# GpSimd takes over the block sums of two edge passes, ScalarE copies them out of PSUM, VectorE takes over the value products

## The chip, the cores and the metric

The kernel runs on one core of a Trainium2 chip. The metric is the device time of one execution in microseconds (us), as the median of several runs. A core has TensorE (PE, with its weight loads shown apart as PEld), VectorE (DVE), ScalarE (ACT), GpSimd (POOL) and SyncE (SP), which here only issues DMAs. The engines run side by side and wait for each other on semaphores.

## The reference, cut to what matters

Four graph layers run over 6250 nodes with 128 channels and 200000 edges. Two of their steps matter here. The attention layer (called gat) computes for every edge

```
e = leaky_relu(a_src[src] + a_dst[dst]);  e = exp(e - m[dst])      # 4 heads
s = segment_sum(e, dst);  out = segment_sum(h[src] * e, dst)      # later divided by s[dst]
```

and the transformer layer (called value in its last step) computes

```
attn_exp = exp(attn - max)                                        # 8 heads
attn_sum = segment_sum(attn_exp, row);  out = segment_sum(attn_exp * v[col], row)
```

so each pass multiplies a gathered row of 128 channels by a weight per head, and sums rows and weights by node.

## The kernel before

The edges are sorted by node and padded so that a group of 256 edges (two tiles of 128, one edge to a partition) belongs to a single block of 128 nodes. There are NG = 832 groups. The function `pass_phase` makes one pass over them. It is called four times, with kind "max", "gat", "logit" and "value"; the change touches the kinds "gat" and "value" alone. In these two the gathered rows were written to DRAM by an earlier pass, and SyncE loads them back in order, four tiles (a quarter of a ring of 16 tiles, two groups) at a time. A quarter is loaded again once `matched` tells that its groups of the round before are through TensorE.

Each engine runs its own loop over the groups, written out 8 groups to an iteration (`turns`). A stage with a lag of 3 works in turn J on group J-3. The order of the stages in the list is the order on the engine, and nothing is reordered. Per group:

- DVE makes two one-hot tiles of 128x128 by comparing a ramp with the node numbers (`make_hot`, L1495).
- In gat, PE turns them (`turn`, L1442), ACT copies them out of PSUM (`turn_hot`, L1404), PE looks up the values of the destination node (`look`, L1452), and four small DVE steps make the score: `sum_scores` L1536, `lean_scores` L1541, `lower_scores` L1546, `bound_scores` L1553. ACT takes the exponential (`exp_scores`, L1408) and DVE multiplies the rows by it (`message`, L1560). PE also runs one matmul whose result nobody reads (`idle`, L1482).
- In value, ACT copies the finished weights beside the rows (`weights`, L1413) and GpSimd multiplies the rows by them (`message`, L1381).
- PE multiplies one-hot by rows (`multiply`, L1476) and leaves a block's 128x132 (gat) or 128x136 (value) sums of this group in a PSUM bank. There are 2 banks for this in gat and 4 in value (`sum_ring`).
- DVE adds the bank to the accumulator `k.acc` in SBUF, at the columns of the group's block (`add`, L1505). It reads the block's number from a table into a register for that (L1293). TensorE waits on `added` before it uses a bank again.

The order on each engine before is: in gat, DVE sum_scores, message, lean_scores, make_hot, lower_scores, add, bound_scores; ACT exp_scores, turn_hot; PE multiply, idle, look, turn. In value, DVE make_hot, add; ACT weights; GpSimd message; PE multiply.

Of the kernel before, what the change touches and what calls it, by code (L numbers as in the profile page):

```python
# [1245 lines left out]
def pass_phase(nc, k, name, which, table, row, kind):  # L1246
# [75 lines left out]
    def wait(eng, sem, count):  # L1322

        if not (isinstance(count, int) and count <= 0):
            eng.wait_ge(sem, count)
# [8 lines left out]
    def ring(j):  # L1334
        return G * (j % GB)


    used = {"logit": scored}.get(kind, matched)

    with nc.Block() as block:  # L1340
        def load_quarter(sp, i, q):
# [31 lines left out]
        @block.gpsimd  # L1373
        def _(pool):
            def message(g, i, j):

                arrived(pool, i, j)
                pool.wait_ge(weighed, g + 1)
                rows = k.gat[:, ring(j):ring(j) + G, 0:C].rearrange("p t (h c) -> p t h c", h=H2)
                wts = k.gat[:, ring(j):ring(j) + G, C:C + H2].unsqueeze(3).to_broadcast([P, G, H2, D2])  # L1380
                pool.tensor_tensor(rows, rows, wts, ALU.mult).then_inc(ready, 1)  # L1381

            if kind == "value":
                turns(pool, [(0, message)])
                return
            if from_lists:
                return
            for first in range(0, T, QUARTER):
                if first >= BODY:
                    pool.wait_ge(used, (first - BODY + QUARTER) // G)  # L1390
                    if keeps:
                        pool.wait_ge(kept[first % BODY // QUARTER], first // BODY * 16)
                    pool.sem_inc(k.passed, 1)
                for m in range(first, first + QUARTER):
                    pool.indirect_dma_start(  # L1395
                        far[:, m % BODY, 0:row], None, table,
                        bass.IndirectOffsetOnAxis(k.idx[:, m:m + 1], axis=0)).then_inc(k.gathered[m % BODY], 16)

        @block.scalar
        def _(act):  # L1400
            def turn_hot(g, i, j):

                act.wait_ge(turned, g + 1)
                act.activation(k.hot_t[:, j % 2, :], tb[j % 2][:, 0:G * P], ACT.Copy).then_inc(copied, 1)  # L1404

            def exp_scores(g, i, j):
                act.wait_ge(scored, g + 1)
                act.activation(k.gat[:, ring(j):ring(j) + G, C:A1], z[:, j % 2, :, :], ACT.Exp).then_inc(weighed, 1)  # L1408

            def weights(g, i, j):  # L1410

                wait(act, matched, g + 1 - GB)
                act.activation(k.gat[:, ring(j):ring(j) + G, C:A2],  # L1413
                               k.big[:, bass.ds((i * BODY + G * j) * H2, G * H2)]
                               .rearrange("p (t h) -> p t h", h=H2), ACT.Copy).then_inc(weighed, 1)

            def diagonals(g, i, j):

                arrived(act, i, j)
                wait(act, matched, g + 1 - MAX_RING)  # L1420
                for t in range(G):
                    for hd in range(H1):
                        if (t, hd) != (G - 1, H1 - 1):
                            last = act.activation(diag[:, j % MAX_RING, t, hd, :], k.ident[:, :], ACT.Copy,  # L1424
                                                  scale=k.gat[:, ring(j) + t, C + hd:C + hd + 1])
                last.then_inc(ready, 1)

            if kind == "sum":
                return
            turns(act, {"max": [(0, diagonals)],  # L1430
                        "gat": [(3, exp_scores), (0, turn_hot)],
                        "logit": [(0, turn_hot)],
                        "value": [(0, weights)]}[kind])

        @block.tensor
        def _(pe):
# [20 lines left out]
            def multiply(g, i, j):  # L1457

                pe.wait_ge(hot, g + 1)
                if kind == "max":  # L1460
                    wait(pe, reduced, g + 1 - MAX_RING)
                else:
                    wait(pe, added, g + 1 - sum_ring)
                if kind == "sum":
                    arrived(pe, i, j)
                else:
                    pe.wait_ge(ready, g + 1)
                if kind == "max":
                    pe.wait_ge(ready_too, g + 1)
                for t in range(G):  # L1470
                    oh = k.oneh[:, ring(j) + t, :]
                    if kind == "max":
                        rhs = diag[:, j % MAX_RING, t, :, :].rearrange("p h c -> p (h c)")
                        last = pe.matmul(k.psum[G * (j % MAX_RING) + t][:, :], oh, rhs, start=True, stop=True)  # L1474
                    else:
                        last = pe.matmul(agg[j % sum_ring][:, 0:width], oh, k.gat[:, ring(j) + t, 0:width],  # L1476
                                         start=(t == 0), stop=(t == G - 1))
                last.then_inc(matched, 1)

            def idle(g, i, j):  # L1480
# [3 lines left out]

            turns(pe, {"gat": [(5, multiply), (5, idle), (2, look), (0, turn)],
                       "logit": [(2, look), (0, turn)],
                       "value": [(1, multiply)]}.get(kind, [(0, multiply)]),
                  )

        @block.vector  # L1490
        def _(dve):
            def make_hot(g, i, j):

                for t in range(G):
                    last = dve.tensor_scalar(k.oneh[:, ring(j) + t, :], k.ramp[:, :],  # L1495
                                             k.loc[:, bass.ds(i * BODY + G * j + t, 1)], None, ALU.is_equal)
                last.then_inc(hot, 1)
# [57 lines left out]
            def message(g, i, j):  # L1555

                dve.wait_ge(weighed, g + 1)
                rows = k.gat[:, ring(j):ring(j) + G, 0:C].rearrange("p t (h c) -> p t h c", h=H1)
                wts = k.gat[:, ring(j):ring(j) + G, C:C + H1].unsqueeze(3).to_broadcast([P, G, H1, D1])
                dve.tensor_tensor(rows, rows, wts, ALU.mult).then_inc(ready, 1)  # L1560

            def multiply_endpoints(g, i, j):
# [28 lines left out]
            if kind == "max":  # L1591
                link(dve, dve.tensor_copy(k.maxa[:, :], k.asrc[:, :, :].rearrange("p b h -> p (b h)")))
            elif width:
                link(dve, dve.memset(k.acc[:, 0:NB * width], 0.0))
            turns(dve, {
                "sum": [(0, make_hot), (2, add)],
                "max": [(2, reduce_peaks), (0, make_hot), (0, diagonal), (2, take_peaks)],
                "gat": [(3, sum_scores), (4, message), (3, lean_scores), (0, make_hot), (3, lower_scores), (6, add),
                        (3, bound_scores)],
                "logit": [(3, multiply_endpoints), (4, scale_logits), (0, make_hot), (4, cut_logits),  # L1600
                          (3, sum_heads)],
                "value": [(0, make_hot), (3, add)]}[kind],
                )


# [583 lines left out]
```

## Time and profile before

| what | value |
|---|---|
| median of 3 runs | 18222.75 us (18222.41 to 18253.24) |
| the profiled execution | 18246.61 us, its span in the trace 18244.7 us |
| gat pass in the span | about 11985 to 13565 us |
| value pass in the span | about 16510 to 17386 us |
| DVE busy over the whole span | 8553.8 us (47%) |
| PE busy over the whole span | 10294.6 us (56%) |

In the rows further below, a group of instructions is named by its line in the kernel, its engine, its operation and the tiles it writes and reads; `room` is the buffer that holds rows, one-hot tiles and work space, `banks` is PSUM, `acc` the accumulator. "PE" rows of a matmul in 32-bit floats show two records for one instruction of the kernel.

### The profile page before, as it was taken

The page shows a single profiled execution, that of the slowest core. Times are in us where ns is not written, and L with a number is a line of the kernel's source. Part 1 is how long each engine was busy: PE and PEld are TensorE (multiplying, and loading weights), DVE is VectorE, ACT ScalarE, POOL GpSimd, SP SyncE. Part 2 cuts the span into 40 slices and gives each one's busy share as a digit, 9 for nine tenths or more (in the row PEclk, how much of TensorE's full clock was granted, in tenths as well). Part 3 has the DMA queues.
Part 4 walks back from the last instruction along what each step waited for, and adds up shares of the span by engine and source line. Part 5 has one row for each costly group of instructions (what it writes and reads, how often), then busy time and mean ns, then how long its engine had stood idle before and what let it go on. Part 6 is the DMA issues. An engine that isn't in the chain of part 4 may idle for free. (4 is left out here: it accounts for less than half of the span.)

```text
span 18244.7 us, 253309 instructions
## 1 busy us (share of the span) xinstructions
PE 10294.6 (56%) x45199; PEld 6926.1 (38%) x45200; DVE 8553.8 (47%) x36079; ACT 3739.1 (20%) x12248; POOL 6911.5 (38%) x7336
## 2 busy tenths in 40 slices
PE   5555555521000566478956666689974444445668
PEld 4444444410000566434422222256663333334544
DVE  6333333320000788831056555577774444448841
ACT  0111111100000122100046666632221111111200
POOL 1444444467777000000035555510005555554500
PEclk8555555555555555588978888899986656668989
DMA  0000000000000566666733333342224444444436
GB/s 22 1 1 1 1 1 1 1 25 1 15 18 18 169 197 196 176 233 230 270 81 85 84 84 84 83 70 72 72 61 121 120 121 120 119 118 110 127 142 223
DMA packets 1812403, 1676.94 MB, mean 92 GB/s; under 512 B 271444, under 2 KB 1664048, under 8 KB 1773712
## 3 DMA queue, kind: packets, MB, share of 16 engines
q1 hardware_dynamic: 1291008, 1199.97, 21.2%
q0 software_dynamic: 234960, 339.86, 8.2%
q10 hardware_dynamic: 286272, 135.29, 2.5%
q8 instruction: 59, 0.97, 0.0%
q14 instruction: 104, 0.85, 0.0%
HBM read 1160.30 MB, written 514.00 MB: 92 GB/s over the span
## 5 line engine op out<-in xcount | busy, mean ns | idle before, releaser
L1395 POOL DMA_INDIRECT room<-tab_h,idx x1664 | 1587.1, 954 | 4401.0 <-POOLq L2133 3302.3
L1395 POOL DMA_INDIRECT acc<-tab_kv,idx x1664 | 1588.7, 955 | 2896.3 <-POOLq L2133 1759.1
L1474 PE MATMUL banks<-acc,room 128*128 128x512 f32 x3328 | 1813.3, 691 | 933.7 <-DVE acc L1511 650.4
L852 POOL DMA_INDIRECT by_src<-big,h x1568 | 1523.6, 972 | 1894.1 <-DVE h L580 1444.5
L1424 ACT ACTIVATE acc<-ident,room 128x128 f32<-128x128 f32 x5824 | 1779.1, 388 | 990.0 <-issue 363.6
L852 POOL DMA_INDIRECT by_dst<-x,h x1568 | 1668.4, 1064 | 535.2 <-issue 499.1
L1495 DVE TENSOR_SCALAR room<-ramp,loc 128x128 f32<-128x128 f32 x6656 | 1838.8, 321 | 53.2 <-issue 49.9
L1146 DVE SCALAR_TENSOR_TENSOR acc<-acc,h,banks 128x128 f32<-128x128 f32 x3966 | 1078.8, 343 | 1493.7 <-remote 1215.2
L1474 PEld LDWEIGHTS banks<-acc,room 128*128 128x128 f32 x3328 | 670.5, 219 | 2075.7 <-issue 1133.4
L1442 PE MATMUL banks<-ident,room 128*128 128x128 f32 x3328 | 861.0, 349 | 1025.6 <-DVE room L1495 628.9
L1476 PE MATMUL banks<-room 128*128 128x132 f32 (+1 forms) x6656 | 1179.5, 309 | 452.1 <-DVE room L1495 190.3
L567 DVE SCALAR_TENSOR_TENSOR room<-banks,room 128x50 f32<-128x50 f32 x3136 | 436.8, 205 | 2122.3 <-remote 1068.9
L1039 PE MATMUL banks<-we2t,idx 128*128 128x8 f32 x3328 | 761.9, 358 | 1051.2 <-ACT idx L1074 522.1
L1519 DVE TENSOR_REDUCE room<-banks 128x4 f32<-128x1024 f32 x832 | 1016.2, 1221 | 568.2 <-PE banks L1474 224.1
L1476 PEld LDWEIGHTS banks<-room 128*128 128x128 f32 x6656 | 925.9, 201 | 734.1 <-issue 310.1
L630 PE MATMUL banks<-room 128*50 128x50 bf16 x1568 | 374.3, 239 | 1447.8 <-ACT room L669 1268.8
L636 PE MATMUL banks<-room 50*128 50x100 f32 x3136 | 1168.9, 474 | 0.0
L1039 PEld LDWEIGHTS banks<-we2t,idx 128*128 128x128 f32 x3328 | 753.6, 331 | 1082.5 <-issue 917.6
L1452 PE MATMUL banks<-h,room 128*128 x3328 | 852.6, 400 | 532.9 <-issue 340.7
L1404 ACT ACTIVATE room<-banks 128x256 f32<-128x256 f32 x1664 | 619.9, 375 | 2473.6 <-DMA big<-cells 1262.4
L1643 PE MATMUL banks<-big,h 128*128 128x448 f32 x2744 | 1037.5, 541 | 16.6 <-DMA big<-cells 16.6
L1566 DVE TENSOR_TENSOR room<-acc,banks 128x256 f32<-128x256 f32 x832 | 348.2, 418 | 1390.6 <-DMA big<-cells 1018.9
(410 smaller groups left out, 15590.2 us busy)
## 6 DMA issues: line engine op xcount, KB each, us to landing
big<-cells SPq DMA_DIRECT2D x262, 1568.0 KB
cells<-acc SPq DMA_DIRECT2D x1985, 64.0 KB, 1.5
cells<-acc ACTq DMA_DIRECT2D x1984, 64.0 KB
head_rows<-room SPq DMA_DIRECT2D x416, 264.0 KB
room<-head_rows SPq DMA_DIRECT2D x416, 264.0 KB, 2.8
acc<-w_rows SPq DMA_DIRECT2D x208, 512.0 KB
value_rows<-acc SPq DMA_DIRECT2D x416, 256.0 KB
room<-value_rows SPq DMA_DIRECT2D x416, 256.0 KB, 2.8
```

Source lines behind the costliest of these rows:

```text
L636: pe.matmul(self.look_bank[g % 2][:, m % 4 * P:m % 4 * P + 2 * NB1], self.turn_sb[g % 2][:, m % 4 * P:(m % 4 + 1) * P], self.tables[m % 4] ...
L852: pool.indirect_dma_start(self.target, bass.IndirectOffsetOnAxis(self.slots[:, t:t + 1], axis=0), self.rec[:, t, :], None).then_inc(self.s ...
L1039: last = pe.matmul(mix[n % 2][:, t * H2:(t + 1) * H2], hid[:, n % 2, t * P:(t + 1) * P], k.we2t[:, :], start=True, stop=True)
L1146: dve.scalar_tensor_tensor(k.cells[:, c * SIDE + m, :], before, k.cell_flag[:, bass.ds(j * (2 * SUB) + s * SUB + c * SIDE + m, 1)], cell_b ...
L1395: pool.indirect_dma_start(far[:, m % BODY, 0:row], None, table, bass.IndirectOffsetOnAxis(k.idx[:, m:m + 1], axis=0)).then_inc(k.gathered[ ...
L1424: last = act.activation(diag[:, j % MAX_RING, t, hd, :], k.ident[:, :], ACT.Copy, scale=k.gat[:, ring(j) + t, C + hd:C + hd + 1])
L1442: last = pe.transpose(tb[j % 2][:, t * P:(t + 1) * P], k.oneh[:, ring(j) + t, :], k.ident[:, :])
L1474: last = pe.matmul(k.psum[G * (j % MAX_RING) + t][:, :], oh, rhs, start=True, stop=True)
L1476: last = pe.matmul(agg[j % sum_ring][:, 0:width], oh, k.gat[:, ring(j) + t, 0:width], start=(t == 0), stop=(t == G - 1))
L1495: last = dve.tensor_scalar(k.oneh[:, ring(j) + t, :], k.ramp[:, :], k.loc[:, bass.ds(i * BODY + G * j + t, 1)], None, ALU.is_equal)
L1519: dve.tensor_reduce(peaks[:, j % 2, :], view, AX.XY, ALU.max).then_inc(reduced, 1)
L1643: pe.matmul(k.psum[b][:, 0:WID], rows[:, src, :], strips[m % ring][:, b * WID:(b + 1) * WID], start=(src == 0), stop=(src == NB - 1)).then ...
```

## The change

In both passes the add leaves DVE. ScalarE gets a new stage `drain`, first in its list: it waits for `matched`, copies the sums from PSUM to one of two SBUF tiles (`shares`), and counts `drained`. GpSimd gets a new stage `add`: it reads the block's number, waits for `drained` and for its own add before, and adds the SBUF tile to `k.acc`. TensorE now waits on `drained` for a free bank. In value, the product of rows and weights leaves GpSimd and becomes DVE's `message`, with the wait for the loaded rows; TensorE's multiply moves from lag 1 to lag 2. DVE's `make_hot` gets a wait on `matched`, which the add's place in DVE's list had made needless.

```diff
+    pool_adds = kind in ("gat", "value")
+    cleared, drained = k.sem(n + "cleared"), k.sem(n + "drained")
+    shares = k.wk[:, 256:256 + 2 * width].rearrange("p (s c) -> p s c", s=2) if pool_adds else None
...
 # GpSimd
+            def add(g, i, j):
+                b = block_number(pool, g, j)
+                pool.wait_ge(drained, g + 1)
+                wait(pool, added, g)
+                mine = k.acc[:, bass.ds(b * width, width)]
+                pool.tensor_tensor(mine, mine, shares[:, j % 2, :], ALU.add).then_inc(added, 1)
+            if pool_adds:
+                pool.wait_ge(cleared, 1)
+                turns(pool, [({"gat": 6, "value": 3}[kind], add)])
+                return
...
 # ScalarE
+            def drain(g, i, j):
+                act.wait_ge(matched, g + 1)
+                wait(act, added, g - 1)
+                act.activation(shares[:, j % 2, :], agg[j % sum_ring][:, 0:width], ACT.Copy).then_inc(drained, 1)
-                        "gat": [(3, exp_scores), (0, turn_hot)],
+                        "gat": [(6, drain), (3, exp_scores), (0, turn_hot)],
-                        "value": [(0, weights)]}[kind])
+                        "value": [(3, drain), (0, weights)]}[kind])
...
 # TensorE
-                    wait(pe, added, g + 1 - sum_ring)
+                    wait(pe, drained if pool_adds else added, g + 1 - sum_ring)
-                       "value": [(1, multiply)]}.get(kind, [(0, multiply)]),
+                       "value": [(2, multiply)]}.get(kind, [(0, multiply)]),
...
 # VectorE, make_hot
+                if pool_adds:
+                    wait(dve, matched, g + 1 - GB)
 # VectorE, message
+                heads = {"gat": H1, "value": H2}[kind]
+                if kind == "value":
+                    arrived(dve, i, j)
                 dve.tensor_tensor(rows, rows, wts, ALU.mult).then_inc(ready, 1)
-                "gat": [(3, sum_scores), (4, message), (3, lean_scores), (0, make_hot), (3, lower_scores), (6, add),
+                "gat": [(3, sum_scores), (4, message), (3, lean_scores), (0, make_hot), (3, lower_scores),
                         (3, bound_scores)],
-                "value": [(0, make_hot), (3, add)]}[kind],
+                "value": [(0, make_hot), (1, message)]}[kind],
```

## Rows read from the trace of the kernel before

**Rows 1.** Busy time by stretch: the gat pass, then the value pass.

```profile
core 0: us, PE busy (x) PEld busy (x) DVE busy (x) ACT busy (x) POOL busy (x), PEclk, DMA share, GB/s
11985.00:13565.00 1580.00, 1410.11 (x9152) 1076.38 (x9152) 1249.09 (x6665) 404.78 (x1665) 0.00 (x0) 0.97 0.29 71
16510.00:17386.00 876.00, 590.09 (x3330) 476.66 (x3331) 764.08 (x2502) 185.26 (x833) 506.52 (x832) 0.93 0.43 125
```

**Rows 2.** Groups of instructions in the gat pass, 12100 to 13500 us.

```profile
L1404 ACT ACTIVATE room<-banks 128x256 f32<-128x256 f32 x746 | 273.2, 366 | 15.9 <-PE banks L1442 15.9
L1505 DVE TENSOR_TENSOR acc<-acc,banks 128x132 f32 x746 | 218.0, 292 | 160.0 <-issue 159.8 <-PE banks L1476 0.2
L1408 ACT ACTIVATE room<-room 128x8 f32<-128x8 f32 x746 | 155.3, 208 | 1021.7 <-DVE room L1553 1021.7
```

**Rows 3.** Timeline of one group in the gat pass: start, length, instruction.

```profile
12804.92 0.48 DVE L1495 TENSOR_SCALAR room<-ramp,loc 128x128 f32<-128x128 f32 x2
...
12805.32 0.15 DVE L1546 TENSOR_TENSOR room<-room,banks 128x8 f32<-128x8 f32 x1
...
12805.46 0.44 PE L1442 MATMUL banks<-ident,room 128*128 128x128 f32 x2
12805.68 0.29 DVE L1505 TENSOR_TENSOR acc<-acc,banks 128x132 f32 x1 [0.21 <-issue]
12805.89 0.17 DVE L1553 TENSOR_SCALAR room<-room 128x8 f32<-128x8 f32 x1
12806.05 0.52 PEld L1476 LDWEIGHTS banks<-room 128*128 128x128 f32 x4 [0.39 <-issue]
12806.08 0.69 PE L1476 MATMUL banks<-room 128*128 128x132 f32 x4 [0.18 <-issue]
...
12806.16 0.16 DVE L1536 TENSOR_TENSOR room<-room,banks 128x8 f32<-128x8 f32 x1
12806.21 0.37 ACT L1404 ACTIVATE room<-banks 128x256 f32<-128x256 f32 x1
12806.33 0.43 DVE L1560 TENSOR_TENSOR room<-room 128x256 f32<-128x256 f32 x1
...
12806.67 0.16 DVE L1541 SCALAR_TENSOR_TENSOR room<-room 128x8 f32<-128x8 f32 x1
12806.75 0.48 DVE L1495 TENSOR_SCALAR room<-ramp,loc 128x128 f32<-128x128 f32 x2
...
12807.70 0.17 DVE L1553 TENSOR_SCALAR room<-room 128x8 f32<-128x8 f32 x1
```

**Rows 4.** Groups of instructions in the value pass, 16600 to 17300 us.

```profile
L1495 DVE TENSOR_SCALAR room<-ramp,loc 128x128 f32<-128x128 f32 x1357 | 493.8, 404 | 12.7 <-issue 11.7
...
L1381 POOL TENSOR_TENSOR room<-room 128x256 f32<-128x256 f32 x678 | 412.6, 629 | 287.5 <-DMA room<-value_rows 201.9 <-ACT room L1413 83.9
...
L1505 DVE TENSOR_TENSOR acc<-acc,banks 128x136 f32 x679 | 198.2, 292 | 67.6 <-PE banks L1476 38.0 <-issue 20.1
L1413 ACT ACTIVATE room<-big 128x16 f32 x679 | 146.5, 216 | 554.0 <-PE banks L1476 554.0
```

**Rows 5.** Timeline of the value pass: GpSimd runs two products while DVE makes one-hot tiles.

```profile
17110.33 1.20 POOL L1381 TENSOR_TENSOR room<-room 128x256 f32<-128x256 f32 x2 [0.59 <-DMA room<-value_rows]
17110.37 1.24 DVE L1495 TENSOR_SCALAR room<-ramp,loc 128x128 f32<-128x128 f32 x2
...
17111.53 0.28 DVE L1505 TENSOR_TENSOR acc<-acc,banks 128x136 f32 x1
17111.74 0.47 DVE L1495 TENSOR_SCALAR room<-ramp,loc 128x128 f32<-128x128 f32 x2
...
17112.13 0.28 DVE L1505 TENSOR_TENSOR acc<-acc,banks 128x136 f32 x1
```

**Rows 6.** Shortest, median and longest instruction (ns) of L1495, L1505 (16600 to 17300 us), L1381.

```profile
L1495 DVE TENSOR_SCALAR room<-ramp,loc x1357: 272/281/750, 16599.8 to 17299.5; 128x128 f32<-128x128 f32 x194
...
L1505 DVE TENSOR_TENSOR acc<-acc,banks x679: 280/295/298, 16600.0 to 17299.8; 128x136 f32 x170
...
L1381 POOL TENSOR_TENSOR room<-room x832: 612/620/742, 16520.5 to 17377.2; 128x256 f32<-128x256 f32 x167
```

**Rows 7.** A group of GpSimd elsewhere, over the whole span: 1984 elements for each partition.

```profile
L818 POOL IOTA acc<- 49x1984 int32 x1 | 3.8, 3840 | 0.0
```

**Rows 8.** The read of a block's number on DVE's sequencer, in the value pass.

```profile
L1293 DVEq TENSOR_LOAD <-block_src x832: 297/304/321, 16524.5 to 17382.0; - x167
```

**Rows 9.** DMA issues in the value pass: KB of each, median us from issue to landing.

```profile
room<-value_rows SPq DMA_DIRECT2D x340, 256.0 KB, 2.8
```

More of the change, by code:

```diff
@@ L1557, in message @@
                 dve.wait_ge(weighed, g + 1)
-                rows = k.gat[:, ring(j):ring(j) + G, 0:C].rearrange("p t (h c) -> p t h c", h=H1)
-                wts = k.gat[:, ring(j):ring(j) + G, C:C + H1].unsqueeze(3).to_broadcast([P, G, H1, D1])
+                heads = {"gat": H1, "value": H2}[kind]
+                rows = k.gat[:, ring(j):ring(j) + G, 0:C].rearrange("p t (h c) -> p t h c", h=heads)
+                wts = k.gat[:, ring(j):ring(j) + G, C:C + heads].unsqueeze(3).to_broadcast([P, G, heads, C // heads])
+                if kind == "value":
+                    arrived(dve, i, j)
                 dve.tensor_tensor(rows, rows, wts, ALU.mult).then_inc(ready, 1)
@@ L1594, in _ @@
                 link(dve, dve.memset(k.acc[:, 0:NB * width], 0.0))
+                if pool_adds:
+                    dve.sem_inc(cleared, 1)
             turns(dve, {
```

## The prediction

> **What bounds the kernel now.** I read the busy time by stretch first, to see what the two passes are worth. They hold 1580 and 876 us of the span [rows 1]; everything else stays as it is. In gat PE is busy for 89% and DVE for 79% of the stretch, GpSimd not at all. In value DVE is busy for 87%, GpSimd for 58%, PE for 67%.
>
> Then I read the timeline of one gat group [rows 3]. From one bound_scores to the next (12805.89 to 12807.70) are 1.81 us. DVE works through its list with two holes: 0.21 us before the add and 0.10 us before sum_scores (12806.06 to 12806.16). PE has one hole, 0.18 us before its multiply. The row calls it "issue", but the weights of that multiply start at 12806.05, 0.08 us after the add ended at 12805.97, and with two banks that add is just what multiply waits for. So DVE sets the pace and PE follows it. The mean is higher than the steady group: 1400 us hold 746 groups [rows 2], 1.877 us each. The 0.06 us above 1.81 are the loop's turn after every 8 groups, which stays.
>
> In value, 700 us hold 679 groups [rows 4]: 1.031 us each. Undisturbed, DVE needs 0.60 us for a group (add to add, 17111.53 to 17112.13, rows 5). The rest, 0.43 us, is the point of this case. While GpSimd runs two products in 1.20 us, DVE's two make_hot instructions take 1.24 us instead of 0.47 and end 0.08 us behind GpSimd's [rows 5]. One make_hot takes 272 ns at least and 750 at most, while the add, which reads one operand from PSUM, stays between 280 and 298 [rows 6] in the same stretch. So a GpSimd tensor_tensor holds up some DVE instructions and not others. GpSimd is hardly held up itself (620 median, 742 longest). The wait of GpSimd for its rows, 201.9 us [rows 4], is no bound: it works ahead of PE by as much as the ring and the 2.8 us of a load [rows 9] let it, and DVE is what is occupied.
>
> **The change part by part.** A "price" below is us per group; there are 832 groups in each pass.
>
> *Gat, the add leaves DVE.* Between the end of lower_scores (12805.32 + 0.15 = 12805.47, rows 3) and the start of bound_scores (12805.89) lie 0.42 us with the add in them. Without it bound_scores must still wait for lower_scores to finish. The nearest row of such a direct dependence is bound_scores to sum_scores, 0.10 us. That takes off 0.32; I count 0.30. DVE's list then takes 1.51 us. PE's hole before multiply goes too, as it waits for drained, an older event; 1.81 - 0.18 = 1.63 is PE's pace by its records, and less if the modelled ends overlap (the idle matmul starts before multiply's recorded end). So between 0.18 and 0.30 are to be had before GpSimd's side is counted.
>
> *Gat, what is added on ACT.* The copy of 128x132 out of PSUM is not in the trace. It lies between exp_scores, 8 elements in 208 ns, and turn_hot, 256 elements in 366 ns [rows 2]; in proportion 208 + 158 x 124/248 = 287 ns. ACT has then 0.21 + 0.37 + 0.29 = 0.87 us of work in a group of 1.5 or more. Behind drain's waits stand exp_scores and turn_hot, and for these DVE's message and PE's look wait. The matched that drain wants is that of PE's turn before, over a microsecond old, so it costs 0; if it were late, exp_scores would be late by as much. Its wait for added is for an add two groups old.
>
> *What is added on GpSimd.* Its add of 132 or 136 elements is not in the trace. From 620 ns for 256 elements [rows 6] and 3840/1984 = 1.94 ns for an element of another GpSimd operation [rows 7] I get 620 - 124 x 1.94 = 380 ns. In bare proportion it would be 320, with no dependence on size 620. Its read of the block number, 0.30 us on DVE's sequencer [rows 8], comes before the waits and so runs beside the add before; with it and the two waits GpSimd needs 0.4 to 0.8 us, under either pace. The Trainium skill (GPSIMD Engine Reference, Elementwise side-by-side cycle accounting) gives about 2.6 cycles of 1.2 GHz per element for such an operation; put in place of 1.94 ns, that 2.17 ns makes the add about 350 ns, an estimate, and the sum is then some 20 us lower.
>
> *What that add costs DVE in gat.* Bounds: nothing, or its whole 0.38. Where it falls can be worked out. Turn starts 0.06 us after the pair of make_hot has ended (12804.92 + 0.48 = 12805.40) and takes 0.44; turn_hot 0.37 follows, then drain 0.29, so the add starts about 1.2 us behind the end of the pair and ends at 1.58. DVE's next pair lies at 1.03 to 1.51. The add thus meets the second make_hot, which should end 0.08 behind it, at 1.66, or 0.15 late. The hand-overs between four engines are not in this and push the add a little further, so I take 0.19, half the add.
>
> Gat: -0.30 + 0.19 = -0.11, times 832 = -92 us. With 0 it is -250 us, with 0.38 it is +67 us.
>
> *Value, DVE's list.* The add leaves: 0.60 becomes the pair alone, 0.39 (17111.74 to 17112.13). The product comes in: message 0.34 in gat from its start to the next (12806.33 to 12806.67, rows 3), with the same 256 elements. Together 0.73, which is +0.13. The block number's read goes to GpSimd. The loads from DRAM stay the same in number and size and now hold up DVE rather than GpSimd if late; with 8 groups of ring, 2.8 us of landing and a pace near 1 us they are not. If that cover went, make_hot behind message would wait as well.
>
> *Value, what the port costs DVE.* Now it is 0.43 for 0.61 us of GpSimd work per group (412.6/678), 0.7 of it. GpSimd's work falls to 0.38. At the same share the loss is 0.27. But in the list before, 0.39 of 0.60 was make_hot and the rest, the add, was immune. Message reads both operands from SBUF; whether it is held up no row shows. If so, all of DVE's list is exposed, and the loss rises to the whole 0.38. Bounds: 0.27 x 0.39/0.73 x 0.60/0.39 = 0.22 and 0.38. I take 0.34, nearer to the full one, as a reader of two SBUF tiles is nearer to make_hot (SBUF to SBUF) than to the add from PSUM.
>
> Value: +0.13 - 0.43 + 0.34 = +0.04, times 832 = +33 us. PE (multiply 0.70), ACT (0.29 + 0.22) and GpSimd stay under 1.07.
>
> The Trainium skill (SBUF State Buffer, Who interferes with whom) says that a VectorE instruction with two SBUF inputs blocks against a GpSimd instruction that reads SBUF, and whichever comes second waits for the whole of the other. The make_hot rows agree as to the blocking [rows 5, 6]; for message no row shows it. By the rule value's loss is 0.38 and the sum 33 us higher. It speaks against this change, as the third case below.
>
> The sum is -92 + 33 = -59 us. Against the profiled execution, 18246.6, it gives 18187.6; the median is 24 us lower, 18222.75, and gives 18163.7. I predict 18164.
>
> **The rivals.** Put as one line, with s and v the loss per group to GpSimd's add in gat and in value, the change is 832 x (s + v - 0.60). My forecast has s + v = 0.53.
>
> *Message is immune.* Then v is 0.22 or less, as the lists can slip past each other, and s stays 0.19: -158 us, 18065, and with s = 0 -316 us. For it speaks that the add in value is immune though it reads SBUF too; against, that both of message's inputs are in SBUF.
>
> *GpSimd's add stops DVE for its full length in both passes.* s = v = 0.38: +133 us, 18356. It decides from s + v = 0.60 on, an average stop of 0.30. For it speaks that two products of 1.20 us pushed make_hot to 1.24 us; against, that in gat small steps with a PSUM operand and holes of 0.10 us stand in DVE's list, during which a stop costs nothing. An add of 620 ns, if its length hardly depends on its size, would lead here as well.
>
> *The two passes cancel.* s + v between 0.56 and 0.64: within 36 us of before. In particular, if gat's PE pace of 1.63 holds, gat gives 0.18 at most, and s only shows above 0.12.
>
> **How the numbers follow.** A measurement of this kernel can tell about 0.2%, 36 us. Chances: forecast (-36 to -150 us) 0.40; message immune or gat undisturbed (beyond -150) 0.18; cancel 0.20; full stop (over +36) 0.22. So faster 0.58, same 0.20, slower 0.22. The range leaves out about a tenth at each end: s + v from 0.30 (-250 us) to 0.72 (+100), which is 17973 to 18323. The likeliest case alone spans 18073 to 18187.
>
> **What would show it.** In the profile after: the gat pass shorter by about 90 us, value longer by about 30; bound_scores 0.1 behind lower_scores; multiply no longer behind a DVE add but right behind turn; drain near 290 ns and GpSimd's add near 380. make_hot's mean in gat rises from 280 to about 370 ns. In value make_hot falls below its 404 ns, and message shows whether it is held up: a mean of 424 says immune, well above says blocked. I am wrong if GpSimd's add takes over 500 ns, if it lands beside steps that are immune, or if ACT's drain makes exp_scores late.

## The result and the profile after

The changed kernel takes 17963.2 us (median of 4 runs, 17951.06 to 17977.92) against 18228.36 us (4 runs) for the kernel before: a ratio of 0.9846, 95% interval 0.9834 to 0.9858, or 265 us less. The forecast was 59 us less. The sign was right, the size was wrong by more than a factor of four, and 17963 lies 10 us under the low end of the range. The profiled execution took 17951.06 us, and its span is 17949.3 us.

Busy time by stretch, gat pass and value pass, to be set against [rows 1]:

```profile
core 0: us, PE busy (x) PEld busy (x) DVE busy (x) ACT busy (x) POOL busy (x), PEclk, DMA share, GB/s
11975.00:13338.00 1363.00, 1250.49 (x9152) 1066.57 (x9152) 1182.16 (x5840) 603.24 (x2499) 447.27 (x832) 0.99 0.34 83
16285.00:17092.00 807.00, 585.97 (x3335) 442.95 (x3335) 793.43 (x2503) 334.27 (x1666) 563.28 (x832) 0.99 0.47 135
```

Gat is 217 us shorter by these stretches (1580 to 1363), value 69 us (876 to 807). The difference of the two spans, 295 us, is all but 9 us in the two passes. DVE has 67 us less of busy time in gat (1249 to 1182), but the pass gains three times that. TensorE's granted clock is a little higher too, 0.99 for 0.97 in gat and for 0.93 in value; in windows inside the passes it is 1.00, and it is 1.00 as well with the short adds below, whose pace is another, so it does not set the pace of the changed kernel.

Groups of the gat pass from 12000 to 13300 us, against [rows 2]:

```profile
L1518 DVE TENSOR_SCALAR room<-ramp,loc 128x128 f32<-128x128 f32 x1616 | 439.1, 314 | 0.0
L1392 POOL TENSOR_TENSOR acc<-acc,room 128x132 f32 x808 | 434.9, 538 | 864.9 <-ACT room L1447 864.9
...
L1586 DVE TENSOR_TENSOR room<-room 128x256 f32<-128x256 f32 x808 | 342.9, 424 | 3.8
...
L1447 ACT ACTIVATE room<-banks 128x132 f32<-128x132 f32 x808 | 222.9, 276 | 10.4
L1576 DVE TENSOR_SCALAR room<-room 128x8 f32<-128x8 f32 x808 | 182.5, 226 | 37.9
```

1300 us hold 808 groups, 1.609 us each, where it was 1.877. The drain (L1447) takes 276 ns, near the 287 that were forecast. GpSimd's add (L1392) takes 538 ns and not 380. The make_hot mean (L1518) is 314 and bound_scores (L1576) 226, which was 166.

Timeline of one gat group, against [rows 3]:

```profile
12701.20 0.43 DVE L1586 TENSOR_TENSOR room<-room 128x256 f32<-128x256 f32 x1
...
12701.39 0.28 ACT L1447 ACTIVATE room<-banks 128x132 f32<-128x132 f32 x1
...
12701.62 0.47 DVE L1518 TENSOR_SCALAR room<-ramp,loc 128x128 f32<-128x128 f32 x2
...
12701.84 0.57 POOL L1392 TENSOR_TENSOR acc<-acc,room 128x132 f32 x1 [0.94 <-ACT room L1447]
12702.02 0.16 DVE L1569 TENSOR_TENSOR room<-room,banks 128x8 f32<-128x8 f32 x1
...
12702.21 0.24 DVE L1576 TENSOR_SCALAR room<-room 128x8 f32<-128x8 f32 x1
...
12702.48 0.21 ACT L1423 ACTIVATE room<-room 128x8 f32<-128x8 f32 x1 [0.81 <-DVE room L1576]
12702.55 0.16 DVE L1559 TENSOR_TENSOR room<-room,banks 128x8 f32<-128x8 f32 x1
...
12702.72 0.43 DVE L1586 TENSOR_TENSOR room<-room 128x256 f32<-128x256 f32 x1
```

Look at where the add lies. It begins 0.22 us into the pair of make_hot, when the second one is already under way, and ends before the next message. The pair keeps its 0.47. Beside the rest of the add stand lower_scores, with an operand in PSUM and no longer than before (154 ns on average, 155 before), and bound_scores, SBUF to SBUF, at 0.24 where it was 0.17. And bound_scores starts 0.03 us after lower_scores ended (12702.18 to 12702.21), not 0.10. From there a chain leads on: exp_scores (L1423) starts 0.03 us after bound_scores has ended, and message (L1586) 0.03 us after exp_scores has. So a longer bound_scores makes message late, while the 0.10 us before sum_scores (L1559) pass beside exp_scores.

This is the steady group, 1.52 us from message to message. It is not every group. In 200 of the 808, two of every eight, near the turn of the loop, the add starts at most 0.016 us after a make_hot and goes first. Then make_hot is the one that is held up, and bound_scores is free:

```profile
12009.74 0.74 DVE L1518 TENSOR_SCALAR room<-ramp,loc 128x128 f32<-128x128 f32 x2
12009.94 0.46 POOL L1392 TENSOR_TENSOR acc<-acc,room 128x132 f32 x1 [1.20 <-ACT room L1447]
...
12010.69 0.17 DVE L1576 TENSOR_SCALAR room<-room 128x8 f32<-128x8 f32 x1
```

Groups of the value pass from 16350 to 17050 us, against [rows 4]:

```profile
L1518 DVE TENSOR_SCALAR room<-ramp,loc 128x128 f32<-128x128 f32 x1485 | 509.9, 383 | 0.0
L1392 POOL TENSOR_TENSOR acc<-acc,room 128x136 f32 x743 | 503.8, 678 | 197.2 <-POOL acc L1392 133.7 <-ACT room L1447 63.4
...
L1586 DVE TENSOR_TENSOR room<-room 128x256 f32<-128x256 f32 x742 | 305.8, 412 | 0.0
```

700 us hold 742 groups, 0.943 us each, where it was 1.031. The timeline of the value pass, against [rows 5]:

```profile
16702.32 0.41 DVE L1586 TENSOR_TENSOR room<-room 128x256 f32<-128x256 f32 x1
16702.36 0.70 POOL L1392 TENSOR_TENSOR acc<-acc,room 128x136 f32 x1 [0.24 <-POOL acc L1392]
...
16702.65 0.69 DVE L1518 TENSOR_SCALAR room<-ramp,loc 128x128 f32<-128x128 f32 x2
...
16703.26 0.41 DVE L1586 TENSOR_TENSOR room<-room 128x256 f32<-128x256 f32 x1
```

Message starts 0.04 us before the add, keeps its 0.41 and looks immune; the add beside it takes 0.70. Then the first make_hot is late: the pair takes 0.69. From these lines alone message could be immune or merely first, which is what the experiments had to tell apart.

### The profile page after: what moved, and what is told of

The parts are those of the page before. It is cut to its first block and busy times, and to the rows that moved or that the text cites. A ratio compares the mean times of both kernels' runs of the same rounds, so it can differ in the third digit from the quotient of the medians.

```text
span 17949.3 us, 259624 instructions
## 1 busy us (share of the span) xinstructions
PE 10136.5 (56%) x45199; PEld 6883.8 (38%) x45200; DVE 8525.5 (47%) x35247; ACT 4084.0 (23%) x13912; POOL 7404.8 (41%) x8169
## 5 line engine op out<-in xcount | busy, mean ns | idle before, releaser
L1495 PE MATMUL banks<-acc,room 128*128 128x512 f32 x3328 | 1819.8, 693 | 930.7 <-DVE acc L1534 604.4
L1518 DVE TENSOR_SCALAR room<-ramp,loc 128x128 f32<-128x128 f32 x6656 | 1859.3, 324 | 45.1 <-issue 41.7
L1392 POOL TENSOR_TENSOR acc<-acc,room 128x132 f32 (+1 forms) x1664 | 1010.6, 607 | 1228.2 <-ACT room L1447 1077.6
L1495 PEld LDWEIGHTS banks<-acc,room 128*128 128x128 f32 x3328 | 672.9, 219 | 2076.9 <-issue 1167.4
L1497 PE MATMUL banks<-room 128*128 128x132 f32 (+1 forms) x6656 | 1106.9, 289 | 262.7 <-DVE room L1586 237.4
L1497 PEld LDWEIGHTS banks<-room 128*128 128x128 f32 x6656 | 881.0, 190 | 427.5 <-DVE room L1518 207.8
```

The source lines that it names most:

```text
L1392: pool.tensor_tensor(mine, mine, shares[:, j % 2, :], ALU.add).then_inc(added, 1)
```

## The experiments

The kernel before took 13839.02, 13835.6, 18289.15 and 18109.56 us in the four series of experiments, each on a chip of its own or at another time. The difference lies in the stages ahead of gat, whose exp_scores begin at 8218.9 us of the span in the first series and at 11987.5 in the trace after. What was not altered in the two passes kept its pace: from the first exp_scores to the last, the changed gat pass takes 1335 to 1340 us in all eight traces that have it, and from the first weights to the last, the changed value pass takes 791 us in all six. So the experiments are read by the pace in a window of a pass: us divided by groups. Gat alone, the changed kernel again and the two kernels with an operand moved to PSUM were timed four or five times, the others once. The kernel before has its trace from the first comparison only.

**Only the gat part of the change.** Value as before.

```diff
-    pool_adds = kind in ("gat", "value")
+    pool_adds = kind == "gat"
...
-                        "value": [(3, drain), (0, weights)]}[kind])
+                        "value": [(0, weights)]}[kind])
...
-                       "value": [(2, multiply)]}.get(kind, [(0, multiply)]),
+                       "value": [(1, multiply)]}.get(kind, [(0, multiply)]),
...
-                "value": [(0, make_hot), (1, message)]}[kind],
+                "value": [(0, make_hot), (3, add)]}[kind],
```

> Only the gat pass has the change; the value pass is that of before (GpSimd multiplies, VectorE adds). Theory (both passes gain, each by itself): the gat pass stays at 1.61 us per group and value returns to 1.03, so the time lies 223 us under before and 73 us over the changed kernel. Rival (the whole gain is gat's and value's shorter stretch is bought by the state in which gat leaves the clock or the DMAs): the time is within 20 us of the changed kernel.

Measured: gat and value pass, windows of 1300 us and of 700 us.

```profile
L1392 POOL TENSOR_TENSOR acc<-acc,room 128x132 f32 x809 | 434.6, 537 | 866.8 <-ACT room L1447 866.8
```

```profile
L1384 POOL TENSOR_TENSOR room<-room 128x256 f32<-128x256 f32 x698 | 422.3, 626 | 279.2 <-DMA room<-value_rows 265.5 <-ACT room L1428 13.6
```

1.607 us per group in gat and 1.003 in value. The gain of gat stands by itself. Value as before is somewhat faster here than the 1.031 of the first trace. By the windows the value part brings 0.06 to 0.09 us per group, 50 to 73 us; from the first weights to the last it is 833 us here and 791 in the run with the drain moved, on the same chip, 42 us, and 856 against 791 in the first comparison, 66 us. The kernel took 0.9818 of the kernel before (0.9794 to 0.9843), 13596.16 us. The changed kernel unaltered, run again:

> The changed kernel unaltered, on the same chip as the experiments, to set its time against theirs: the passes at 1.61 and 0.94 us per group as before, and 1.6 to 2.1% under the kernel before on this chip.

It took 17997.41 us, 0.9837 of the kernel before (0.9824 to 0.9851), in agreement with the first comparison.

**What the add still costs in gat.**

```diff
-                mine = k.acc[:, bass.ds(b * width, width)]
-                pool.tensor_tensor(mine, mine, shares[:, j % 2, :], ALU.add).then_inc(added, 1)
+                cols = 8 if kind == "gat" else width
+                mine = k.acc[:, bass.ds(b * width, cols)]
+                pool.tensor_tensor(mine, mine, shares[:, j % 2, 0:cols], ALU.add).then_inc(added, 1)
```

> The changed kernel, but in the gat pass GpSimd adds only the first 8 of the 132 columns (the other columns of the sums are left out). It measures what the add still costs in gat. Theory (0.03 to 0.06 us per group): the pace goes from 1.61 to 1.55 to 1.59. Rival (nothing at all, the pace is that of VectorE's and TensorE's own lists): 1.60 to 1.62.

Measured, 12050 to 13250 us:

```profile
L1519 DVE TENSOR_SCALAR room<-ramp,loc 128x128 f32<-128x128 f32 x1602 | 382.9, 281 | 0.0
...
L1393 POOL TENSOR_TENSOR acc<-acc,room 128x8 f32 x801 | 187.1, 234 | 1013.4 <-ACT room L1448 1013.4
```

1200/801 = 1.498 us per group. The add costs 0.11 more than a short one, more than this expectation had and less than the 0.19 of the forecast. make_hot is back at 281 ns and bound_scores at 172, so the short add leaves no mark on either. The two account for the 0.11 within 0.01: bound_scores was 0.05 longer on average (226 for 172 ns), the two make_hot together 0.07 (314 for 281 each).

**The place of the add in gat.**

```diff
-                        "gat": [(6, drain), (3, exp_scores), (0, turn_hot)],
+                        "gat": [(3, exp_scores), (6, drain), (0, turn_hot)],
```

> The changed kernel, with gat's drain between exp_scores and turn_hot, so that GpSimd's add starts about 0.4 us earlier against VectorE's list and falls beside message, lean_scores and the first make_hot. Theory (gat loses almost nothing because the add lies beside instructions that it cannot stop): the pace goes from 1.61 to between 1.70 and 1.95 us per group, 75 to 280 us for the pass, with a make_hot mean well above 314 ns. Rival (GpSimd's add hardly stops anything in gat, wherever it lies): the pass stays within 15 us.

Measured, 8300 to 9600 us, and two lines of the timeline:

```profile
L1392 POOL TENSOR_TENSOR acc<-acc,room 128x132 f32 x728 | 362.7, 498 | 938.1 <-ACT room L1447 938.1
...
L1564 DVE SCALAR_TENSOR_TENSOR room<-room 128x8 f32<-128x8 f32 x728 | 261.9, 360 | 0.0
...
L1559 DVE TENSOR_TENSOR room<-room,banks 128x8 f32<-128x8 f32 x728 | 118.3, 163 | 151.6 <-PE banks L1473 103.4
```

```profile
9000.21 0.75 DVE L1518 TENSOR_SCALAR room<-ramp,loc 128x128 f32<-128x128 f32 x2
9000.22 0.47 POOL L1392 TENSOR_TENSOR acc<-acc,room 128x132 f32 x1 [1.28 <-ACT room L1447]
```

1300/728 = 1.786 us per group, 0.18 slower for the same work (145 us for the pass). The add meets lean_scores, which reads the same SBUF tile as both of its operands and rises from 160 to 360 ns, or the pair of make_hot, 0.75 instead of 0.47. The position of one instruction in ScalarE's list is worth two thirds of what the gat part brings. Not all of it is the stop, though. turn_hot now stands behind the drain, so TensorE's look comes later, and sum_scores (L1559) waits for it: the idle time before sum_scores rose from 0.15 to 0.21 us per group (122.9 us over 808 groups, 151.6 over 728). One part of the expectation failed: the make_hot mean stays at 311 ns, since lean_scores takes the stop.

**Is it VectorE's list, or TensorE's banks?** ScalarE drains, VectorE adds the copy, GpSimd is idle in gat.

```diff
-                turns(pool, [({"gat": 6, "value": 3}[kind], add)])
+                if kind == "value":
+                    turns(pool, [(3, add)])
...
-                dve.wait_ge(matched, g + 1)
+                dve.wait_ge(drained if kind == "gat" else matched, g + 1)
...
-                dve.tensor_tensor(mine, mine, agg[j % sum_ring][:, 0:width], ALU.add).then_inc(added, 1)
+                share = shares[:, j % 2, :] if kind == "gat" else agg[j % sum_ring][:, 0:width]
+                dve.tensor_tensor(mine, mine, share, ALU.add).then_inc(added, 1)
...
-                "gat": [(3, sum_scores), (4, message), (3, lean_scores), (0, make_hot), (3, lower_scores),
+                "gat": [(3, sum_scores), (4, message), (3, lean_scores), (0, make_hot), (3, lower_scores), (6, add),
```

> Gat with drain on ScalarE as in the changed kernel, but VectorE adds the copy in SBUF, at the add's old place; GpSimd idle; value as changed. Theory (gat gains because the add and the register read before it leave VectorE's list): 1.80 to 1.88 us per group, so at most 60 of the 223 us remain. Rival (gat gains because TensorE gets its banks back from ScalarE and no longer waits on VectorE's add): 1.61 to 1.70 us per group.

Measured, 8300 to 9700 us:

```profile
L1530 DVE TENSOR_TENSOR acc<-acc,room 128x132 f32 x734 | 217.7, 297 | 171.3 <-issue 166.4 <-ACT room L1448 5.0
```

1400/734 = 1.907 us per group: no faster than before (1.877), and above the range of the theory too. TensorE has its banks early and gains nothing. The gain is that of VectorE's list. With the add in it, 0.42 us lie between the end of lower_scores and the start of bound_scores (0.23 us of idle time on average, then the add); without it 0.03.

**Value with a short add.**

```diff
-                mine = k.acc[:, bass.ds(b * width, width)]
-                pool.tensor_tensor(mine, mine, shares[:, j % 2, :], ALU.add).then_inc(added, 1)
+                cols = 8 if kind == "value" else width
+                mine = k.acc[:, bass.ds(b * width, cols)]
+                pool.tensor_tensor(mine, mine, shares[:, j % 2, 0:cols], ALU.add).then_inc(added, 1)
```

> The changed kernel, but in the value pass GpSimd adds only the first 8 of the 136 columns of a group's sums (the other columns of the sums are left out). Theory (the pace of value is set by GpSimd's add together with what it stops on VectorE): the pace falls from 0.94 us per group to 0.75 to 0.85, 75 to 160 us, and make_hot returns near 280 ns. Rival (value is set by the loop from ready over multiply and drain, or by the loads): it stays within 0.03 us of 0.94.

Measured, 11900 to 12400 us:

```profile
L1519 DVE TENSOR_SCALAR room<-ramp,loc 128x128 f32<-128x128 f32 x1376 | 321.9, 272 | 0.0
L1587 DVE TENSOR_TENSOR room<-room 128x256 f32<-128x256 f32 x688 | 281.4, 409 | 0.0
L1393 POOL TENSOR_TENSOR acc<-acc,room 128x8 f32 x688 | 280.1, 407 | 220.3 <-POOL acc L1393 169.5 <-ACT room L1448 50.8
```

500/688 = 0.727 us per group. That is DVE's list alone, 0.39 + 0.34 = 0.73 in the forecast. The full add costs 0.943 - 0.727 = 0.216 us more than the short one.

**Value without GpSimd.** VectorE multiplies and adds.

```diff
-    pool_adds = kind in ("gat", "value")
+    pool_adds = kind == "gat"
...
-                "value": [(0, make_hot), (1, message)]}[kind],
+                "value": [(0, make_hot), (1, message), (4, add)]}[kind],
```

> Value without any GpSimd or ScalarE share in the sums: VectorE makes one-hot tiles, multiplies (lag 1) and adds from PSUM (lag 4); gat as in the changed kernel. Theory (a VectorE instruction costs its own issue and nothing stops it): 0.39 + 0.34 + 0.22 + 0.06 = 1.01 us per group, between before (1.03) and after (0.94), with make_hot at 280 ns. Rival (the hand-overs between engines cost more than the port): 0.95 or less, as fast as the changed kernel.

Measured, a stretch of the timeline:

```profile
12300.53 0.42 DVE L1583 TENSOR_TENSOR room<-room 128x256 f32<-128x256 f32 x1
...
12301.00 0.30 DVE L1525 TENSOR_TENSOR acc<-acc,banks 128x136 f32 x1
...
12301.80 0.42 DVE L1583 TENSOR_TENSOR room<-room 128x256 f32<-128x256 f32 x1
...
12302.44 0.30 DVE L1525 TENSOR_TENSOR acc<-acc,banks 128x136 f32 x1 [0.22 <-issue]
```

1.144 us per group (699 groups in 800 us), the slowest of all. From message's start to the add's are 0.47 us in the first of these groups and 0.64 in the second, and not 0.34: the add, whose column comes from a register, costs VectorE 0.42 in all (1.144 - 0.727), twice the 0.21 us from its start to the next instruction's. Neither theory had this. On VectorE's sequencer the read of the block's number takes 0.31 us and begins at 12301.83, just after message has started, and the add follows at 12302.44. The hole of 0.21 us before the add in gat [rows 2] has the same order of events. No run has such an add without the read, so that the read is the cause is likely and not shown.

**Value with two accumulators.**

```diff
-                wait(pool, added, g)
+                wait(pool, added, g - 1 if kind == "value" else g)
                 mine = k.acc[:, bass.ds(b * width, width)]
+                if kind == "value" and j % 2:
+                    mine = k.h[:, :, :].rearrange("p b c -> p (b c)")[:, bass.ds(b * C, C)]
+                    pool.tensor_tensor(mine, mine, shares[:, 1, 0:C], ALU.add).then_inc(added, 1)
+                    return
```

> Value with two accumulators: GpSimd adds odd groups into a second one (128 columns, without the 8 weights, and it is not used afterwards, so the sums of the odd groups are left out), so an add waits only for the add two groups back. Theory A (value is set by GpSimd's chain of one add after the other, 0.70 us and 0.24 us of waiting for itself): the pace falls from 0.94 to 0.80 to 0.87 us per group. Theory B (value is set by the time that GpSimd's add and VectorE's instructions with two SBUF operands or two ports cannot share): it stays at 0.92 to 0.96, with GpSimd waiting for ScalarE instead of for itself.

Measured, 11950 to 12650 us:

```profile
L1590 DVE TENSOR_TENSOR room<-room 128x256 f32<-128x256 f32 x725 | 395.5, 546 | 0.0
```

0.966 us per group: a little slower (Theory B had at most 0.96), though GpSimd hardly waits for its own adds any more. Theory A falls. And now message takes 546 ns on average: in half of the groups its 0.41 us, and in the other half, where the add comes 0.09 to 0.18 us before it, 0.69. As soon as the add can come first, message is the one that is held up.

**What each does to the other.** Four extra stages.

```diff
+                other = {"sbuf": hh[:, 256:512], "psum": k.psum[0][:, 0:256]}[second]
+                dve.tensor_tensor(k.big[:, m * 256:(m + 1) * 256], hh[:, 0:256], other, ALU.mult).then_inc(done, 1)
...
+                pool.tensor_tensor(k.big[:, 4096 + m * 136:4096 + (m + 1) * 136], k.acc[:, 0:136],
+                                   k.acc[:, 136:272], ALU.add).then_inc(done, 1)
...
+        run(probe_phase, "sbuf", 16, 0)      # 16 products on VectorE
+        run(probe_phase, "sbuf", 0, 16)      # 16 adds on GpSimd
+        run(probe_phase, "sbuf", 16, 16)     # both
+        run(probe_phase, "psum", 16, 16)     # both, VectorE's second operand in PSUM
```

> The changed kernel with four short extra stages at its end, each 16 instructions per engine: VectorE products of 256 elements from two SBUF operands alone; GpSimd adds of 136 elements alone; both at once; and both at once with VectorE's second operand in PSUM. They measure what each does to the other. Theory (two SBUF operands and a GpSimd add exclude each other): in the third stage the spacing of VectorE's products rises from 0.34 us towards the sum with an add, 0.7 or more, or the adds grow longer, while in the fourth both keep the spacing that they have alone. Rival (only the one-hot comparison is stopped, message is immune): third and fourth stage alike.

Measured, the timeline of the four stages:

```profile
13519.04 5.46 DVE L2161 TENSOR_TENSOR big<-h 128x256 f32<-128x256 f32 x16 [0.89 <-PEq L2181]
13525.21 6.87 POOL L2167 TENSOR_TENSOR big<-acc 128x136 f32<-128x136 f32 x16 [853.35 <-ACTq L2156]
13532.82 9.64 POOL L2167 TENSOR_TENSOR big<-acc 128x136 f32<-128x136 f32 x16 [0.74 <-ACTq L2156]
13532.84 9.90 DVE L2161 TENSOR_TENSOR big<-h 128x256 f32<-128x256 f32 x16 [8.34 <-PEq L2181]
13543.44 6.89 POOL L2167 TENSOR_TENSOR big<-acc 128x136 f32<-128x136 f32 x16 [0.98 <-ACTq L2156]
13543.45 5.39 DVE L2161 TENSOR_TENSOR big<-h,banks 128x256 f32<-128x256 f32 x16 [0.71 <-PEq L2181]
```

Alone, 16 products take 5.46 us and 16 adds 6.87. Together with both operands in SBUF they take 9.90 and 9.64: they alternate, one product, one add. With the second operand in PSUM they take 5.39 and 6.89, as if each were alone. So message is not immune. But both together take 9.90 and not the sum of 12.33: an add adds (9.90 - 5.46)/16 = 0.28 us to VectorE's list, well below the 0.43 us from one add to the next.

**Message without its second SBUF operand.** ScalarE writes the value weights into PSUM too.

```diff
...
+                act.activation(apart(j), k.big[:, bass.ds((i * BODY + G * j) * H2, G * H2)], ACT.Copy)\
+                    .then_inc(weighed, 1)
...
+                    wts = apart(j).rearrange("p (t h) -> p t h", h=H2).unsqueeze(3).to_broadcast([P, G, H2, D2])
```

> The changed kernel, and in the value pass ScalarE writes the weights a second time, into PSUM, and message takes them from there, so that it has one SBUF operand only. Theory (a VectorE product with two SBUF operands and GpSimd's add exclude each other, one with a PSUM operand and the add do not): the add shrinks from 0.70 us to below 0.60, the pace of value falls from 0.94 to 0.80 to 0.88 us per group, 50 to 115 us for the pass. Rival (the stop of make_hot is all that counts, and message's operands do not matter): the pace stays at 0.92 to 0.96.

Measured, 16350 to 16900 us:

```profile
L1524 DVE TENSOR_SCALAR room<-ramp,loc 128x128 f32<-128x128 f32 x1456 | 369.0, 294 | 0.0
L1396 POOL TENSOR_TENSOR acc<-acc,room 128x136 f32 x728 | 343.6, 472 | 206.6 <-POOL acc L1396 160.9 <-ACT room L1453 45.7
L1593 DVE TENSOR_TENSOR room<-room,banks 128x256 f32<-128x256 f32 x728 | 298.9, 411 | 0.0
```

550/728 = 0.755 us per group, below what was expected, and 0.03 above VectorE's list. Seven groups of eight take 0.72 us, that list alone; at the turn of the loop a make_hot meets the add, and the group takes 0.97. The add is down to 472 ns, make_hot to 294. The kernel takes 17839.26 us, 0.976 of the kernel before (0.9747 to 0.9774) on the chip where the changed one takes 0.9837.

**bound_scores without its SBUF output.** On top of that, in gat.

```diff
-                act.activation(k.gat[:, ring(j):ring(j) + G, C:A1], z[:, j % 2, :, :], ACT.Exp).then_inc(weighed, 1)
+                act.activation(k.gat[:, ring(j):ring(j) + G, C:A1], z(j), ACT.Exp).then_inc(weighed, 1)
...
-                dve.tensor_scalar(z[:, j % 2, :, :], sums, 0.0, None, ALU.min).then_inc(scored, 1)
+                dve.tensor_scalar(z(j), sums, 0.0, None, ALU.min).then_inc(scored, 1)      # z(j) in PSUM bank 3
```

> The kernel with the weights in PSUM, and in the gat pass bound_scores writes its 8 values into PSUM (bank 3, which the idle matmul gives up) and exp_scores reads them there. bound_scores takes 226 ns on average beside GpSimd's add and 172 with a short add. Theory (its two SBUF sides are what the add stops): it returns to about 175 ns and gat's pace falls from 1.61 to 1.54 to 1.57 us per group, 30 to 55 us for the pass. Rival (what gat still pays is the make_hot that meets the add): 1.59 to 1.62, bound_scores at 175 or not.

Measured, 12000 to 13000 us:

```profile
L1525 DVE TENSOR_SCALAR room<-ramp,loc 128x128 f32<-128x128 f32 x1332 | 340.1, 297 | 0.0
L1397 POOL TENSOR_TENSOR acc<-acc,room 128x132 f32 x666 | 321.6, 483 | 679.4 <-ACT room L1454 679.4
...
L1428 ACT ACTIVATE room<-banks 128x8 f32<-128x8 f32 x665 | 118.2, 178 | 473.3 <-DVE banks L1583 473.3
L1583 DVE TENSOR_SCALAR banks<-room 128x8 f32<-128x8 f32 x666 | 113.0, 170 | 31.3
```

1000/666 = 1.502 us per group, the pace of the short add. It beats the expectation for two reasons. Fewer make_hot meet the add (297 for 314 ns). And exp_scores (L1428), which now reads PSUM, takes 178 ns where it took 208; as message waits for it, that is 0.03 us of the 0.11 and has nothing to do with GpSimd. The kernel takes 17580.94 us, 0.9705 of the kernel before (0.9692 to 0.9719), 1.8 times the gain of the changed kernel run again (0.9837). It is the best version found.

## Why the prediction was wrong

The order of the sum held: VectorE's list is what changes in both passes, and what is left over is GpSimd's add stopping VectorE. The sizes of three terms failed.

*"Gat, the add leaves DVE", 0.30.* It was 1.877 - 1.498 = 0.38. I kept 0.10 us for the wait of bound_scores for lower_scores, from bound_scores and sum_scores. The timeline shows 0.03. sum_scores waits for two further semaphores, the loaded rows and the look, so it was not such a bare pair. The steady list takes 1.45 us when undisturbed, not 1.51, and TensorE's pace of 1.63 "by its records" was no floor: its recorded ends overlap the next start. With that the rival in which TensorE caps gat's gain at 0.18 falls.

*"What that add costs DVE in gat", 0.19.* It was 1.609 - 1.498 = 0.11. The place was right: the add starts 1.2 to 1.3 us behind the end of a pair, in the second half of the next one. But I had it stop the second make_hot without asking which of the two starts first. In three groups of four make_hot does, in the one shown by 0.03 us (12701.62 + 0.47 - 0.28 = 12701.81, the add at 12701.84). Then the add waits, ends later (0.57 for its 0.46), and lies beside lower_scores, which reads PSUM, and bound_scores, which it makes 0.07 longer. In the other quarter the add goes first and make_hot takes 0.55 for 0.28. Over all groups that is 0.75 x 0.07 + 0.25 x 0.27 = 0.12, the measured 0.11. The forecast's case is thus the rarer one, and its sum had no term for bound_scores. Which of the two comes first is a matter of 0.02 us; where the forecast came near here, that was luck. With both terms gat gave -0.27 for -0.11, which is 131 us of the miss.

*"Value, what the port costs DVE", 0.34.* It was 0.216. The list was right to 0.003 us (0.727). I took 0.9 of a whole add of 0.38. The add is longer than that (0.47 alone, 0.68 in this pass), but what it takes from VectorE at a stop is 0.22 to 0.28 us, and the bound that I had called the lower one, 0.22, was the truth. The share that the term started from was read too high as well: I put all of 0.43 us down to GpSimd's product, but the rows show 2 x (404 - 281) = 0.25 us of longer make_hot [rows 4, 6] and (67.6 + 12.7)/679 = 0.12 us of idle time before the add and make_hot [rows 4]. That is 0.4 of GpSimd's 0.61 us and not 0.7. Value gave -0.09 for +0.04, 106 us of the miss, and there the forecast had the sign wrong; that the sum had it right is gat's doing.

GpSimd's add was mis-sized too, 0.38 us for the 0.47 that it takes undisturbed, as the step from 256 elements down to 136 was 0.15 us and not 0.24. It was to be a sign of being wrong on the slow side (over 500 ns), and it came true (538 and 678 ns) while the kernel was faster than forecast. The aside with 350 ns for the add does not fit the prediction's own shares: half of 0.03 in gat and 0.9 of it in value are some 35 us, not 20. Nothing else rests on it.

The rival "message is immune" came nearest in time but not by its reason. Message and the add exclude each other (9.90 us for 5.46), in value message is merely first each time and hands the delay to the add and the next make_hot. The full-stop rival fell: s + v was 0.11 + 0.22 = 0.33, where it decides from 0.60 on. With the 0.08 that gat's list gave beyond the forecast, the forecast's own line reads 832 x (0.33 - 0.68) = -291 us, against 295 between the two spans. The medians are 265 us apart: the profiled execution of the changed kernel lies 12 us below its median, that of the kernel before 18 us above.

The Trainium skill (SBUF — State Buffer, Who interferes with whom) names two SBUF inputs as a condition for such a block, and the four stages agree: 9.90 us with two, 5.39 with one in PSUM. It is not the only condition here: make_hot and bound_scores read one SBUF tile element by element and were stopped as well (0.28 to 0.55 us, 0.17 to 0.24). The Trainium skill also has the later one wait for all of the other; by the lengths of the stages it waited for less, 0.28 of 0.43 us.

Still open: why an instruction's recorded length holds more than the time in which it excludes the other, what the wait before an add with a register in its address consists of, and why value's old arrangement ran at 1.031 us per group in the first comparison and 1.003 in the first series of experiments.

## What to carry to other kernels

When work moves to GpSimd, look not at how long its instruction is but at what VectorE runs beside it: here an operand or a result in PSUM freed VectorE's instruction from the stop, and one small operand or result moved to PSUM gave back (0.943 - 0.755) x 832 = 156 us in one pass and (1.609 - 1.502) x 832 = 89 us in the other, 0.03 of those 0.107 us by a shorter exp_scores. The order of ScalarE's list decides beside which instruction the stop falls, and that was worth up to 0.18 us per group. A mean over a window can hide two kinds of group: look at both before you explain it. And the price of an instruction is read best by leaving it out: an add with a register in its address cost VectorE 0.38 to 0.42 us per group, where its record says 0.29.

## What was not expected of the hardware

- A GpSimd add takes 234 ns for 8 elements (gat with the short add) and 472 for 136 (value, message's second operand in PSUM), so about 1.9 ns for each further element; in value, beside a message with both operands in SBUF, the add of 8 elements read as 407 ns.
- When GpSimd's add and a make_hot start together, 0.02 us decide. With the add up to 0.016 us behind in the records make_hot took 0.55 us and the add 0.46; from about there on make_hot kept its 0.28 and the add took 0.57 to 0.59.
- A VectorE instruction that needs the result of the one just before it started 0.03 us after that one's end in gat (lower_scores to bound_scores), but 0.10 from bound_scores to sum_scores, which has two more semaphores to wait for. Across engines, exp_scores and message each started 0.03 us after the end of what they waited for.
- A VectorE product and a GpSimd add that follow each other every 0.34 and 0.43 us when alone, and that exclude each other, alternate in 0.62 us, 0.15 less than the sum.
